# A fixed first tile per expert, filler and tile table made inside attention, expert results added to the tokens by indirect transfers

## What is computed

```
def _moe(x, rw, rb, w1, b1, w2, b2):            # T = 2048 tokens, D = 256, FF = 1024, E = 8, K = 2
    xf = x.reshape(T, D)
    router_weights = softmax(xf @ rw + rb)
    topw, topi = top_k(router_weights, K)
    topw = softmax(topw)
    combine = zeros((T, E)).at[arange(T)[:, None], topi].add(topw)
    h = gelu(einsum('td,edf->etf', xf, w1) + b1[:, None, :], approximate=False)
    eo = einsum('etf,efd->etd', h, w2) + b2[:, None, :]
    return einsum('etd,te->td', eo, combine)
out = layernorm(x + _moe(x, ...), ln3_g, ln3_b)
```

## Time and profile before

| | us |
|---|---|
| median of 3 runs | 1319.58 (1318.32 to 1324.58) |
| the profiled execution, its own time | 1318.77 |
| the profiled execution, its span | 1317.1 |
| TensorE busy | 1093.4 (83%) |
| VectorE busy | 834.6 (63%) |
| ScalarE busy | 647.5 (49%) |
| GpSimd busy | 451.1 (34%) |

### The profile page before, as it was taken

One profiled execution on the slowest core, in us unless ns is written; L12 is line 12 of the kernel. 1 busy time (PEld: TensorE's weight loads), 2 busy tenths in 40 slices (PEclk: granted clock), 3 DMA queues, 4 the chain that ended last, 5 costly groups with the idle time before them and its releaser, 6 DMA issues. The chain is left out here.

```text
span 1317.1 us, 25953 instructions
## 1 busy us (share of the span) xinstructions
PE 1093.4 (83%) x8912; PEld 897.4 (68%) x8912; DVE 834.6 (63%) x1808; ACT 647.5 (49%) x1384; POOL 451.1 (34%) x694
## 2 busy tenths in 40 slices
PE   2589899999999999999989888888239999999910
PEld 1367677767777777877766656554239999999910
DVE  5456566775554444445678778764348887788846
ACT  1145556565555544445555545445037666766600
POOL 2245555432211223334555133322312321222266
PEclk9799999999999999999999999989569999999965
DMA  3768475754434334444748455631186677766743
GB/s 107 97 105 162 84 95 74 98 105 58 52 48 57 50 49 49 82 50 62 86 65 101 72 81 87 86 56 41 60 309 223 218 229 237 242 209 228 241 132 112
DMA packets 95139, 151.46 MB, mean 115 GB/s; under 512 B 11584, under 2 KB 80704, under 8 KB 88128
## 3 DMA queue, kind: packets, MB, share of 16 engines
q1 hardware_dynamic: 90416, 139.68, 51.7%
q0 software_dynamic: 3392, 9.44, 2.3%
q10 hardware_dynamic: 1232, 1.07, 0.2%
HBM read 82.51 MB, written 16.78 MB: 75 GB/s over the span
## 5 line engine op out<-in xcount | busy, mean ns | idle before, releaser
L742 ACT ACTIVATE probs<-s 128x384 f32<-128x384 f32 (+1 forms) x512 | 267.8, 541 | 291.3 <-PE s L578 278.4
L809 DVE TENSOR_REDUCE neg_max<-s 128x2 f32<-128x512 f32 x256 | 167.7, 688 | 104.1 <-PE s L557 97.3
L807 DVE TENSOR_REDUCE neg_blocks<-s 128x3 f32<-128x384 f32 x256 | 134.8, 555 | 153.4 <-PE s L554 148.0
L578 PE MATMUL s<-q_stack,k_stack 98*128 98x256 bf16 (+1 forms) x1024 | 175.5, 262 | 7.7 <-ACT probs L742 5.6
L458 POOL TENSOR_SCALAR_AFFINE_SELECT probs<-probs 128x256 f32<-128x256 f32 x256 | 104.1, 415 | 181.2 <-ACT probs L742 179.8
L1106 POOL CAST e_w_hi<-e_w 128x512 fp32r<-128x512 f32 x92 | 70.8, 810 | 214.3 <-PE moe L1150 202.8
L578 PEld LDWEIGHTS s<-q_stack,k_stack 98*128 98x128 bf16 x1024 | 90.3, 98 | 41.6 <-ACT probs L742 17.7
L597 PE MATMUL pv<-probs,v 128*32 128x256 f32 (+1 forms) x2048 | 113.3, 363 | 4.8 <-POOL probs L458 4.5
L1150 PE MATMUL moe<-rows_hi,e_w_hi 128*128 128x256 f32 x368 | 105.9, 288 | 11.4 <-DVE rows_lo L1285 11.4
L504 PE MATMUL work<-hT,w_qk 128*128 128x256 f32 x384 | 98.7, 403 | 16.3 <-ACTq L677 16.3
L557 PE MATMUL s<-k_stack,q_stack 96*128 96x256 bf16 x512 | 96.4, 280 | 17.2 <-DVE neg_max L809 16.9
(11 more groups left out here) (175 smaller groups left out, 2446.8 us busy)
## 6 DMA issues: line engine op xcount, KB each, us to landing
e_w<-in_expert_w SPq DMA_DIRECT2D x50, 1024.0 KB, 5.4
k_stack<-k_part SPq DMA_DIRECT2D x192, 128.0 KB, 4.6
q_stack<-q_part SPq DMA_DIRECT2D x192, 128.0 KB, 6.6
rows<-slots_x SPq DMA_DIRECT2D x25, 256.0 KB, 3.4
slots_y<-result SPq DMA_DIRECT2D x23, 256.0 KB, 5.2
cT<-in_context SPq DMA_DIRECT2D x16, 256.0 KB, 6.0
e_b<-in_expert_b SPq DMA_DIRECT2D x24, 128.0 KB, 5.0
x<-in_x SPq DMA_DIRECT2D x8, 256.0 KB, 5.7
```

What stands on the lines that cost most here:

```text
L578: last = pe.matmul(dst[:, kt * S:kt * S + S - q0], k[:, kt * P:(kt + 1) * P], q[:, q0:S], start=True, stop=True)
L742: act.activation(probs[hd][:, 0:width], s2[hd % 2][:, 0:width], ACT.Exp, scale=SCALE).then_inc(probs_ready, 1)
L807: dve.tensor_reduce(neg_blocks[:, :, hd], src[:, 0:3 * P].rearrange("p (b s) -> p b s", b=3), AX_X, ALU.max, negate=True).then_inc(s1_free, 1)
L809: dve.tensor_reduce(neg_max[:, :, hd], src[:].rearrange("p (t s) -> p t s", t=TILES), AX_X, ALU.max, negate=True).then_inc(s1_free, 1)
```

## The change

It has four parts.

1. **Tiles.** Tiles 0 to 7 are now the first 256 slots of experts 0 to 7, whatever the counts; the table covers the other 15 only. The first two tiles' experts and rows are constants. `w1`, `w2` of expert 0 and the bias table are fetched during attention (fetch step "expert"), into buffers that both blocks share.
2. **Into attention.** The table (`tiles_of_experts`) is worked out at the end of VectorE's attention program. The unused slots get filler rows with a token number past the real ones: `fill` on SP, after the ranks of lane 5 (8 register loads, 8 transfers of 512 rows) and of lane 6 (8 and 256 rows). VectorE waits in lane 6's `give_slots` for the first fill. The two shares of a token are computed per lane (`share`: two steps each on VectorE and ScalarE) and travel in the row with its token number and its experts: a row has 261 elements (1044 bytes) in place of 256. The scatter of a lane waits for its shares too.
3. **Results.** `slots_y`, the gathers and `x_all` are gone. GpSimd multiplies a tile's result by the share of each row and adds it to `x_rows` by two indirect transfers that accumulate (`compute_op=ALU.add`), each tile's after the one before has landed. VectorE gets a step `row_data` per tile (3 instructions: the row's token number and its share), which first waits until the transfers of tile n-2 have landed. Since it reads `rows`, the rows of tile n+2 are now fetched after it, and so behind `w2` of tile n+2 in SP's order.
4. **Last norm.** Each lane's tokens are loaded back (8 transfers of 256 KB), and the norm is spread: statistics on VectorE, inverse root on GpSimd, scale and offset on ScalarE, gain on GpSimd (a multiply of 128x512), shift on VectorE, with buffers for all lanes.

At the start of the expert block both tiles are transposed before `up(0)` in place of one. In planned time the shares are due at 69.0 to 71.4 of a unit, between the rank (67.1) and the scatter and the fill (both 72.0). The hunks below are, in order: the scatter on GpSimd, the plan, the shares on VectorE, SP's start and loop in the expert block, `add_rows` and the loop on GpSimd, `row_data` on VectorE, the start on TensorE, and the last norm on GpSimd.

```
+                pool.wait_ge(shares_ready, lane + 1)
+                if lane == B - 1:
+                    pool.wait_ge(filled_rows, 16 + 2 * FILLED)
                 pool.sem_inc(gate, 1)
                 for i in range(TILES):
                     for j in range(TOP):
-                        pool.indirect_dma_start(slots_x, bass.IndirectOffsetOnAxis(ap=slot_of[:, j, lane * TILES + i:lane * TILES + i + 1], axis=0), x[lane][:, i, :], None).then_inc(scattered, 16)
+                        pool.indirect_dma_start(slots_x, bass.IndirectOffsetOnAxis(ap=slot_of[:, j, lane * TILES + i:lane * TILES + i + 1], axis=0), x_row[lane][:, i, :], None).then_inc(scattered, 16)
...
+        steps += [(AT["shares"] + 0.8 * i, "share", lane, i) for i in range(4)]
+        if lane in (B - 3, B - 2):
+            steps += [(AT["fill"], "fill", lane, FINAL)]
...
+            def share(lane, i):
+                shares = x_row[lane][:, :, SHARE:SHARE + TOP]
+                if i == 1:
+                    dve.wait_ge(exps_ready, 2 * lane + 1)
+                    dve.tensor_reduce(total[:], gap[:], AX_X, ALU.add)
+                    dve.drain()
+                    dve.reciprocal(total[:], total[:])
+                    dve.tensor_tensor(ratio[:], gap[:, :, 1], gap[:, :, 0], ALU.subtract)
+                    dve.drain()
+                    dve.tensor_tensor(ratio[:], ratio[:], total[:], ALU.mult).then_inc(gaps_ready, 1)
+                elif i == 3:
+                    dve.wait_ge(exps_ready, 2 * lane + 2)
+                    dve.tensor_scalar(total[:], ratio[:], 1.0, None, ALU.add)
+                    dve.drain()
+                    dve.reciprocal(shares[:, :, 0], total[:])
+                    dve.drain()
+                    dve.tensor_tensor(shares[:, :, 1], ratio[:], shares[:, :, 0], ALU.mult).then_inc(shares_ready, 1)
+                    dve.drain()
...
+            fetch_rows(0, 0)
+            fetch_first(1, 1)
+            fetch_rows(EXPERT_TILES, 1)
+            fetch_bias(0, 0)
+            fetch_second(1, 1)
+            fetch_bias(1, 1)
...
+            step(0, 0, 2)
+            next_rows(0, 0, 2 * EXPERT_TILES)
             with sp.Fori(0, PAIRS) as j:
                 for i in (1, 0):
                     n = j * 2 + 2 - i
                     e, next_e, at = expert(n + 2), expert(n + 1), source(n + 2)
-                    step(n, i, e, at)
-                    write(n - 1, 1 - i)
+                    step(n, i, e)
+                    next_rows(n, i, at)
+                    sp.wait_ge(result_ready, n)
                     fetch_bias(next_e, 1 - i)
...
+            def add_rows(n, i, nth):
+                pool.wait_ge(result_ready, n + 1)
+                pool.sem_inc(gate, 1)
+                pool.tensor_tensor(result[i][:], result[i][:], share[i][:].unsqueeze(2).to_broadcast([P, GT, D]), ALU.mult)
+                pool.drain()
+                pool.wait_ge(added[1 - i], ADDED * nth)
+                pool.sem_inc(gate, 1)
+                for m in range(GT):
+                    pool.indirect_dma_start(x_rows, bass.IndirectOffsetOnAxis(ap=token[i][:, m:m + 1], axis=0), result[i][:, m, :], None, compute_op=ALU.add).then_inc(added[i], 16)
...
                     pool.wait_ge(up_full, n * QUARTERS + 1)
-                    second_high(i, j + 2 - i)
+                    second_high(i, j + 1)
+                    add_rows(n - 1, 1 - i, j + 2 - i)
...
+            def row_data(i, nth):
+                dve.wait_ge(added[i], ADDED * nth)
+                dve.tensor_copy(token[i][:], rows[i][:, :, TOKEN].bitcast(U32))
+                then(dve.scalar_tensor_tensor(out=shares[:], in0=rows[i][:, :, EXPERT:EXPERT + TOP], scalar=b1_e[i][:, FC:FC + 1], in1=rows[i][:, :, SHARE:SHARE + TOP], op0=ALU.is_equal, op1=ALU.mult))
+                dve.tensor_reduce(share[i][:], shares[:], AX_X, ALU.add).then_inc(row_data_ready, 1)
...
             turn(0, 0, 1)
+            turn(1, 1, 1)
             up(0, 0)
-            turn(1, 1, 1)
...
+                pool.tensor_tensor(var_eps[b][:], mean_var[b][:, :, 1], eps[:], ALU.add)
+                pool.drain()
+                pool.tensor_tensor(rstd[b][:], var_eps[b][:], minus_half[:], ALU.pow).then_inc(rstd_ready, 1)
                 if b >= 1:
-                    inverse_root(b - 1)
+                    pool.wait_ge(normal_ready, b)
+                    pool.tensor_tensor(z[b - 1][:], z[b - 1][:], gain[:].unsqueeze(1).to_broadcast([P, TILES, D]), ALU.mult).then_inc(scaled, 1)
```

More of the change, by code:

```diff
@@ L64 @@
       "weigh1": 50.3, "turn": 52.5, "out_T": 54.8, "wo": 57.0, "ffn_ln": 59.5, "ffn_T": 63.0, "ffn_bias": 66.3, "up": (67.2, 73.6, 75.1, 77.0),
-      "down": (80.0, 81.0), "final_ln": 59.2, "final_T": 63.0, "store": 63.5, "router": 65.5, "rank": 67.1, "scatter": 72.0}
+      "down": (80.0, 81.0), "final_ln": 59.2, "final_T": 63.0, "store": 63.5, "shares": 69.0, "fill": 72.0, "router": 65.5, "rank": 67.1, "scatter": 72.0}
 PACE = {"max": 0.7, "head": 1.06}
@@ L853, in choose @@
                 dve.drain()
[L854 removed]
+                ordered = top[:]
+                index_f = x_row[lane][:, :, EXPERT:EXPERT + TOP]
                 for i in range(TILES):
@@ L1191, in first_high @@
             def first_high(i, nth, q):
-                if q == 0:
+                if q == 0 and nth is not None:
                     act.wait_ge(w1_loaded[i], 16 * nth)
@@ L1231, in _ @@
                 for i in (1, 0):
-                    step(j * 2 + 2 - i, i, j + 2)
+                    n = j * 2 + 2 - i
+                    step(n, i, j + 2 - i)
+                    rows_high(n + 1, 1 - i)
+            for b in range(B):
+                act.wait_ge(offset_ready, b + 1)
+                for m in range(TILES):
+                    last = act.activation(z[b][:, m, :], z[b][:, m, :], ACT.Identity, scale=rstd[b][:, m:m + 1], bias=offset[b][:, m:m + 1])
+                last.then_inc(normal_ready, 1)
         @block.vector
@@ L1339, in _ @@
                 first_low(0, 0, q)
-            shares()
+            fetch_bias(0, 0)
+            fetch_bias(1, 1)
             rows_low(0, 0)
-            step(0, 0)
-            result_places()
+            rows_low(1, 1)
+            for q in range(QUARTERS):
+                first_low(1, 1, q)
+                hidden_low(0, 0, q)
+            for q in range(QUARTERS):
+                second_low(0, 0, q)
+            row_data(0, 1)
             with dve.Fori(0, PAIRS) as j:
@@ L1346, in _ @@
                     n = j * 2 + 2 - i
-                    step(n, i)
+                    fetch_bias(n + 1, 1 - i)
+                    for q in range(QUARTERS):
+                        first_low(n + 1, 1 - i, q)
+                        hidden_low(n, i, q)
+                    rows_low(n + 1, 1 - i)
+                    for q in range(QUARTERS):
+                        second_low(n, i, q)
+                    row_data(i, j + 2 - i)
                     add_bias(n - 1, 1 - i, j + 1)
```

421 lines of the change are left out of this document (185 added, 236 removed).

## The result

The changed kernel takes 1352.06 us (median of 4 runs, 1343.85 to 1353.42), the kernel before took 1319.43 in the same comparison: a ratio of 1.0226, with a 95% interval of 1.0185 to 1.0268. It is **slower by 32.6 us**; 1308 was forecast, and the time lies outside the range. The profiled execution took 1353.42 us, its span is 1350.1 against 1317.1, so 33.0 us have to be found.

What follows compares the result with a forecast made beforehand. TensorE was taken to bound the expert loop, the order of waits the last attention call. Terms +9.5 +2.2 -13 +10.5 +3 -24 sum to -11.8 us, giving 1308 us; range 1290 to 1336, forecast case 1302 to 1316.

Steps and rivals of the forecast that it cites:

- Attention, +9.5: Last attention call: shares delay scatter, inverse root and VectorE's apply; half of the delay counted, +9.5 us, bounds 0 and 22.
- The fill: SP's filler rows from lane 5's rank on, 4.3 MB in 14 to 19 us: counted at nothing, 3 us at worst.
- Last lane, +2.2: After the last lane's rank the scatter waits for the shares: +2.2 us, bounds 1.5 and 4.
- start, -13: Start of the expert block: second rows land at E+6.4, third turn begins at E+36.2 where it was 49.2: -13 us.
- E: The time at which the expert block begins, 950.76 in the kernel before.
- +10.5: Expert loop: rows fetched behind w2 land late, two turns take 24.7 us in place of 23.8: +10.5 us.
- +3: Expert loop: adding transfers delay the rows by 0.3 us per pair of turns: +3 us, ends 0 and 15.
- Slow adds: Rival, expert loop: row_data waits for tile n-2's adds, deciding from 7.4 us to landing; about 1350 us, chance 0.13.
- Tail, -24: Last product to the end: 37.6 us where it was 61.9, GpSimd's root and gain setting the pace: -24 us.
- the signs that it gave for being wrong: row_data waits for the adds, transposes never wait, or attention ends where it did or over 20 us later.

Runs made afterwards that it cites:

- the late scatter: Changed kernel with the scatter due at 76.5 of a unit in place of 72.0, behind the next inverse roots: 1326.54 us; two further kernels add other edits to it.
- the wait alone: Kernel before, with the scatter also waiting for a mark that VectorE sets at 71.4 of the unit, without work for it: 1324.75 us.
- the first experiment: Kernel before with only SP's order changed, rows of tile n+2 fetched behind w2 and not ahead of w1: 1330.1 us.

## Why the prediction was wrong

*Attention, +9.5 forecast, +30.7 measured: the step that failed first.* Its mechanism was named and is right (the scatter waits for the shares, the inverse root stands behind it, the apply behind that), and the runs with the late scatter (24.6 us back) and with the wait alone (10.8 us lost) show it from both sides. What failed is "The lane has 5.5 us in which TensorE is idle, so I take half". It allowed 4.2 us per lane as the upper end and took 2.1; lanes 0 to 2 lost 3.8, 8.5 and 4.5. TensorE's idle time was no cover for a delay of VectorE. Even the upper bound was short, for the whole term (22 against 30.7) and for the second of these lanes; that a late root pushes the maxima and with them the next lane's work is my reading, which no run takes apart. Lanes 3 to 6 were taken at the added work alone, 3.2 us in all; they lost 16.1, through the same order of waits and the fill (the first rank came 2.4 us earlier than before, hence 30.7 and not 33). The fill, counted at nothing and 3 us at worst, cost some 4 to 6 us behind lane 5's rank (47.8 us from there to the last rank, 45.2 and 41.6 in the kernel before with shares, with and without the fill): GpSimd stood idle for 4.9 us ahead of lane 6's root. With the scatter behind the roots it costs nothing that can be seen (36.3 to 36.5 us from lane 5's rank to the last in the three kernels with the late scatter).

*Last lane, +2.2 forecast, +1.6 measured; start, -13.* Both right. SP issues the first rows at 983.04 and the third turn begins at E+35.4, forecast E+36.2, by the wait at its place:

```profile
983.04 0.39 SPq L1105 DMA_DIRECT2D rows<-slots_x  x1
983.99 0.43 SPq L1105 DMA_DIRECT2D rows<-slots_x  x1
989.19 1.12 PE L1215 MATMUL moe<-ident,rows 128*128 128x128 f32 x4 [2.19 <-DMA rows<-slots_x]
```

The second rows land and are turned at 989.2, E+6.2 (they were to land at E+6.4).

*Loop, +10.5 and +3 forecast; measured, with the start's gain set against it, some +36.* The +10.5 is right to 0.1 us per pair, by the first experiment, which shows 24.79. By the fit of the Trainium skill (DMA: Bandwidth & Descriptors, "Anatomy of one DMA"), which the page gives for transfers that GpSimd issues, the pair would have been 23.9, an estimate; these are SP's, and the trace does not agree: the 5.2 us row of the same queue was nearer. The step that failed is "GpSimd has 68.5 of 269 us busy and its 1.3+2.6 us more per turn do not fill it". That GpSimd does not fill up is true (155 of 291 us). But the sum asked only whether the engine has room and not what its work does to VectorE when its order changes. The casts moved to directly behind the adding transfers, and there they hold VectorE for 2.4 to 3.2 us, which is worth 2.4 us per pair: `second_low` ends later, `w2` and the rows behind it are fetched later, and the transposes wait (13 times, 19.8 us of TensorE). The +3 for adds that delay the rows was never seen by itself; plain writes in place of the adds gave back 1.3 us per pair. Sizes that were off besides: an add occupies GpSimd for 1.6 to 2.1 us (1.3 forecast) and lands in 6.9 in the loop (3 to 4 forecast).

*Slow adds.* The rival decided from 7.4 us on; the adds stay just below, and `row_data` waits for them once, 0.6 us:

```profile
DVE token L1336 <- DMA x_rows<-result,token: 0.6, 1, 0.6
PEld moe L1215 <- DMA rows<-slots_x: 22.7, 14, 2.2
```

That the time came out near that rival's 1350 is chance: it did so by two other mechanisms. Once the turns are shorter, as with the casts on ScalarE, the waits it spoke of appear, 13 of them.

*Tail, -24 forecast, -21.9 measured.* The order is the one forecast, GpSimd's root and gain in turn, 2.5 us per lane (2.7 forecast). The last tile's adds wait for those before them and start 5.5 and 7.4 us behind the last product, so SP reads the first tokens back at +11.3 in place of +7.0; some 2 of these 4.3 us came back behind it, in the shorter rounds above all:

```profile
1315.49 1.57 POOL L1175 DMA_INDIRECT x_rows<-result,token  x1 [1.87 <-DMA x_rows<-result,token]
1317.36 1.58 POOL L1175 DMA_INDIRECT x_rows<-result,token  x1 [0.30 <-issue]
...
1330.45 1.26 POOL L1203 TENSOR_TENSOR z<-z,ln_gain 128x512 f32<-128x512 f32 x1
```

Of the signs that it gave for being wrong, one came true in full: attention ended over 20 us later. `row_data` did wait for the adds, but once and for 0.6 us.

## What to carry to other kernels

When a change adds a wait to an engine that works in a fixed order, follow what stands behind the waiting instruction to the end of the stage, and count the delay in full for each round as the upper end, unless a slack on that very chain is shown; another engine's idle time is none. Here 2.7 us more of waiting per lane cost 10.8 us over the call, and 4.5 us with the shares' work 24.4. A due time moved by a few units can decide over the whole feature: here 4.5 units gave 24.6 us. When work is added to an engine that is far from full, ask also what now runs directly behind what, and which other engine that touches.

## What the hardware showed that was not expected

- Casts on GpSimd (128x512, four in a row) and VectorE's operations on two SBUF tensors alternate where they meet in the kernels without indirect transfers in the loop: 1.09 us for VectorE, 0.92 to 1.03 per cast. Directly behind indirect transfers the casts often run through in 2.3 to 3.4 us, and a VectorE operation of 0.69 us takes 1.9 to 3.2.
- An adding indirect transfer of 128 KB holds GpSimd for 1.6 to 2.1 us, a plain one for 0.96 to 1.04 in most cases (up to 1.6), and they land after 6.9 and 5.8 us in a loop whose DMA share is 0.68. In the tail, without weights under way, the last adding one was issued at 1317.36 and the tokens were read back from 1321.22 on, 3.9 us later.
- With the fill in flight, GpSimd stood idle for 3.5 to 4.9 us ahead of lane 6's inverse root behind the scatter; at the same place without a fill it was 0.47 us in the kernel before and 1.50 us with late scatters. Up to 3.2 us also occur ahead of a root with no fill under way (behind lane 1's scatter in the changed kernel).
- After a wait of 2 us for rows the granted clock of the 14 us around it is 0.88, where it was 1.00: part of it ran at 1.2 GHz. Its 88 matmuls took 11.96 us, and at the 0.119 us each of the 14 us ahead (118 in 14.00) they would have taken some 10.4, an estimate. A wait cost TensorE more than its length.
